# Attention and wave layer on one core: value matmuls one key tile at a time, overlapping PSUM bank ranges, and the layer norm's last step on VectorE

## What is computed

```python
def layernorm(x):                       # over the 256 columns, no gain or shift
    return (x - mean(x)) / sqrt(var(x) + 1e-5)

def attn(x):                            # 16 heads of 16, causal, rotary positions
    Q, K, V = split(x @ w_qkv); Q, K = rope(Q), rope(K)
    p = softmax(where(causal, Q @ K.T * 16 ** -0.5, -1e9))
    return (p @ V) @ w_proj + b_proj

def ffn(x):
    real = x @ cos(theta + theta_noise); imag = x @ sin(phi + phi_noise)
    return sqrt(real ** 2 + imag ** 2)

x = x + attn(layernorm(x))
x = x + ffn(layernorm(x))
```

## Time and profile before

| | |
|---|---|
| median of 3 runs | 2079.31 us (2078.74 to 2079.62) |
| the profiled execution | 2079.31 us, span from first to last instruction 2077.5 us |
| granted TensorE clock, mean | 0.992 |
| TensorE busy | 2033.7 us, 98% of the span |
| VectorE, ScalarE, GpSimd busy | 1486.1 us (72%), 1400.4 us (67%), 871.2 us (42%) |
| DMA | 159.91 MB, mean 77 GB/s |

### The profile page before, as it was taken

How to read it: one execution, slowest core, us unless ns; L and a number is a source line. 1 busy time by engine, 2 the same in 40 slices (tenths; PEclk the granted TensorE clock), 3 DMA queues, 4 the chain that set the end, 5 groups by cost and what they waited for, 6 DMA issues and landing times.

```text
span 2077.5 us, 39248 instructions
## 1 busy us (share of the span) xinstructions
PE 2033.7 (98%) x13184; PEld 883.4 (43%) x13184; DVE 1486.1 (72%) x2724; ACT 1400.4 (67%) x2705; POOL 871.2 (42%) x1336
## 2 busy tenths in 40 slices
PE   7999999999999999999999999999999999999998
PEld 5433344344443444444443444434444344434345
DVE  4766988877777777786777767787676877778322
ACT  2456667776667676776667676787666766676673
POOL 3335325453433535543363443447344343721242
PEclk9999999999999999999999999999999999999999
DMA  5314222222222322222232222333222222320221
GB/s 144 80 33 110 63 75 72 83 85 71 66 79 69 95 76 72 87 83 87 66 86 80 82 64 66 91 93 95 81 65 73 66 85 76 109 64 13 64 95 36
DMA packets 120553, 159.91 MB, mean 77 GB/s; under 512 B 30746, under 2 KB 82586, under 8 KB 120346
## 3 DMA queue, kind: packets, MB, share of 16 engines
q1 hardware_dynamic: 118480, 154.18, 25.6%
q10 hardware_dynamic: 1872, 3.21, 0.9%
HBM read 88.89 MB, written 50.85 MB: 67 GB/s over the span
## 4 chain that ended last, share of the span: by engine, by line
PE 85%; ACT 5%; issue 3%; POOL 2%; DMA 2%; DVE 2%; SPq 1%; ACTq 0%; POOLq 0%; DVEq 0%
PE banks L938 22%; PE banks L953 21%; PE banks L916 21%; PE banks L871 6%; PE banks L882 5%; PE banks L914 3%; PE banks L898 3%; PE banks L834 3%; ACT probs L1049 2%; DVE chunk_max L1195 2%; DMA stack_k<-split 1%; PE banks L961 1%; PE banks L823 1%; ACT inverse L1069 1%; POOL guess L1272 1%
## 5 line engine op out<-in xcount | busy, mean ns | idle before, releaser
L1195 DVE TENSOR_REDUCE chunk_max<-banks 128x1 f32<-128x512 f32 (+3 forms) x2240 | 1345.7, 667 | 416.2 <-PE banks L916 414.3
L1049 ACT ACTIVATE probs<-banks 128x512 f32<-128x512 f32 (+1 forms) x2240 | 1131.1, 600 | 394.5 <-PE banks L938 270.4
L916 PE MATMUL banks<-stack_k,stack_q 96*128 96x512 bf16 (+3 forms) x2560 | 749.7, 352 | 5.7 <-DVE chunk_max L1195 2.2
L938 PE MATMUL banks<-stack_q,stack_k 99*128 99x512 bf16 (+3 forms) x2560 | 730.5, 350 | 13.4 <-ACT probs L1049 9.2
L953 PE MATMUL banks<-probs,v_one 128*17 128x512 f32 (+3 forms) x5120 | 517.1, 531 | 0.4 <-POOL probs L1337 0.2
L938 PEld LDWEIGHTS banks<-stack_q,stack_k 99*128 99x128 bf16 x2560 | 232.0, 97 | 417.3 <-ACT probs L1049 263.1
L916 PEld LDWEIGHTS banks<-stack_k,stack_q 96*128 96x128 bf16 x2560 | 243.5, 98 | 242.3 <-DVE chunk_max L1195 89.7
L1337 POOL TENSOR_SCALAR_AFFINE_SELECT probs<-probs 128x512 f32<-128x512 f32 x256 | 161.0, 639 | 377.4 <-ACT probs L1049 376.0
L953 PEld LDWEIGHTS banks<-probs,v_one 128*17 128x17 f32 x5120 | 124.9, 97 | 289.9 <-issue 212.6
L914 PE MATMUL banks<-diag_mask,ident_bf 128*128 128x128 bf16 x1024 | 201.2, 223 | 5.4 <-DMA stack_k<-split 3.9
L1321 POOL TENSOR_SCALAR max_neg<-row_max 128x16 f32<-128x16 f32 x64 | 16.4, 257 | 360.6 <-DVE row_max L1204 356.6
(11 more groups left out here) (134 smaller groups left out, 1196.6 us busy)
## 6 DMA issues: line engine op xcount, KB each, us to landing
split<-parts SPq DMA_DIRECT2D x64, 384.0 KB, 2.7
stack_q<-split SPq DMA_DIRECT2D x384, 64.0 KB, 2.3
stack_k<-split SPq DMA_DIRECT2D x354, 64.0 KB, 2.2
sums<-o_raw SPq DMA_DIRECT2D x64, 256.0 KB, 2.1
rot<-raw SPq DMA_DIRECT2D x246, 64.0 KB, 2.0
xin<-x SPq DMA_DIRECT2D x16, 512.0 KB, 4.0
heads_t<-sums SPq DMA_DIRECT2D x26, 256.0 KB
mid<-x SPq DMA_DIRECT2D x13, 512.0 KB, 4.1
```

Source lines behind the costliest of these rows:

```text
L916: mm = nc.tensor.matmul(bank[:, n * wide:(n + 1) * wide], stack_q[u % 2][0:SPLIT_ROWS, t, h + n, j * P:(j + 1) * P], stack_k[u % 2][0:SPLI ...
L938: mm = nc.tensor.matmul(bank[:, a * wide:(a + 1) * wide], stack_k[u % 2][0:ROWS, j // SUB, first + a, (j % SUB) * P:(j % SUB + 1) * P], st ...
L1049: nc.scalar.activation(probs[:, g % PROBS, first:first + many, w0:SPAN], bank, ACT.Exp).then_inc(s_exp, 1)
L1195: nc.vector.tensor_reduce(to, bank[:, 0:count * wide].rearrange("p (h n) -> p h n", h=count), AX.X, ALU.max).then_inc(s_emptied["DVE"], 1)
```

## The change

Three things change together; the plan is then made anew from the same rules, so all queues come out in another order.

1. `VALUES` goes from 2 to 1: a `values` job covers one step, and the exponentials of step g are planned to wait for the values of step g-4 alone instead of the pair.
2. `SCORE_BANKS` goes from banks 0 to 2 to banks 0 to 3, `OTHER_BANKS` from 3 to 6 to 2 to 6. There are still seven banks in the ring; banks 2 and 3 may hold either kind.
3. The last step of both layer norms moves from ScalarE (scale and shift) to VectorE (subtract the mean, multiply by the inverse deviation). VectorE also adds the epsilon, so GpSimd has five operations a block instead of eight.

```diff
-VALUES = 2
+VALUES = 1
-STAT_OPS = 8
-ROOT_OPS = 8
+STAT_OPS = 9
+ROOT_OPS = 5
-SCORE_BANKS = range(0, 3)
-OTHER_BANKS = range(3, 7)
+SCORE_BANKS = range(0, 4)
+OTHER_BANKS = range(2, 7)
...
-            job(("stats", n), "DVE", 2.0, at, ...)
-            job(("dev", n), "POOL", 2.8, at, [("stats", n), ("apply", n - 1)])
-            job(("apply", n), "ACT", 1.35, at, [("dev", n)])
+            job(("stats", n), "DVE", 2.1, at, ...)
+            job(("dev", n), "POOL", 2.0, at, [("stats", n), ("apply", n - 1)])
+            job(("apply", n), "DVE", 1.4, at, [("dev", n)])
...
-                def normalise(n):
-                    half = n % 2
-                    act.wait_ge(s_root, ROOT_OPS * (n + 1))
-                    for j in range(SUB):
-                        ins = nc.scalar.activation(xin[:, half, j, :], xin[:, half, j, :], ACT.Identity, bias=shift[:, j:j + 1], scale=rstd[:, j:j + 1])
-                    ins.then_inc(s_xn, 1)
...
                 def block_stats(n):
                     half = n % 2
                     base = STAT_OPS * n
-                    if n:
-                        dve.wait_ge(s_stat, base)
...
+                    dve.wait_ge(s_stat, base + 8)
+                    nc.vector.tensor_scalar(variance[:, half, :], mv[:, half, :, 1], EPS, None, ALU.add).then_inc(s_stat, 1)
+
+                def normalise(n):
+                    half = n % 2
+                    dve.wait_ge(s_root, ROOT_OPS * (n + 1))
+                    for j in range(SUB):
+                        ins = nc.vector.tensor_scalar(xin[:, half, j, :], xin[:, half, j, :], mv[:, half, j, 0:1], rstd[:, j:j + 1],
+                                                      ALU.subtract, ALU.mult)
+                    ins.then_inc(s_xn, 1)
...
-                    nc.gpsimd.tensor_scalar(var, mean_var[:, :, 1], EPS, None, ALU.add).then_inc(chain, 1)
-                    nc.gpsimd.tensor_scalar(centre[:, :], mean_var[:, :, 0], -1.0, None, ALU.mult).then_inc(chain, 1)
...
-                    nc.gpsimd.tensor_tensor(shift[:, :], centre[:, :], result[:, :], ALU.mult).then_inc(chain, 1)
```

More of the change, by code:

```diff
@@ L224, in plan @@
             job(("xload", n), "SP", 0.45, at, [("xt", n - 2, 1), ("rot", 0, n - 2) if n < SPANS else begun(at - SLACK)], (4.8, 9.5)[n] if n < 2 else 4.2)
-            job(("stats", n), "DVE", 2.0, at, [("xload", n), ("apply", n - 2), *([("apply", 0)] if n == 1 else []), begun(at - SLACK)])
-            job(("dev", n), "POOL", 2.8, at, [("stats", n), ("apply", n - 1)])
-            job(("apply", n), "ACT", 1.35, at, [("dev", n)])
+            job(("stats", n), "DVE", 2.1, at, [("xload", n), ("apply", n - 2), *([("apply", 0)] if n == 1 else []), begun(at - SLACK)])
+            job(("dev", n), "POOL", 2.0, at, [("stats", n), ("apply", n - 1)])
+            job(("apply", n), "DVE", 1.4, at, [("dev", n)])
             for k in range(KT):
@@ L305, in plan @@
                     with_bank(("proj", n, a), ("proj", n, a), "DVE", 0.65, at + 0.1, [("out", ("lead", n, a))])
-            job(("stats3", n), "DVE", 2.0, at + 0.1, [("out", ("proj", n, 1)), ("apply3", n - 1)])
-            job(("dev3", n), "POOL", 2.8, at + 0.1, [("stats3", n), ("apply3", n - 1)])
-            job(("apply3", n), "ACT", 1.35, at + 0.1, [("dev3", n)])
+            job(("stats3", n), "DVE", 2.1, at + 0.1, [("out", ("proj", n, 1)), ("apply3", n - 1)])
+            job(("dev3", n), "POOL", 2.0, at + 0.1, [("stats3", n), ("apply3", n - 1)])
+            job(("apply3", n), "DVE", 1.4, at + 0.1, [("dev3", n)])
             for k in range(KT):
@@ L1096, in _ @@
                         lift(*name[1:])
[L1097 to L1100, removed]
                     elif name[0] == "sin":
@@ L1134, in block_stats3, with normalise3 @@
                         nc.vector.bn_aggr(mv3[:, j, :], stats3[:, j, :]).then_inc(s_stat3, 1)
+                    dve.wait_ge(s_stat3, base + 8)
+                    nc.vector.tensor_scalar(variance3[:, :], mv3[:, :, 1], EPS, None, ALU.add).then_inc(s_stat3, 1)
+                def normalise3(n):
+                    dve.wait_ge(s_root3, ROOT_OPS * (n + 1))
+                    for j in range(SUB):
+                        ins = nc.vector.tensor_scalar(normed3[finish_set(n)][:, j, :], mid[finish_set(n)][:, j, :], mv3[:, j, 0:1], rstd3[:, j:j + 1],
+                                                      ALU.subtract, ALU.mult)
+                    ins.then_inc(s_xn3, 1)
                 def invert(n):
@@ L1243, in _ @@
                         block_stats(name[1])
+                    elif kind == "apply":
+                        normalise(name[1])
                     elif kind == "rope":
@@ L1289, in deviation @@
                     pool.wait_ge(s_stat, STAT_OPS * (n + 1))
-                    inverse_deviation(ROOT_OPS * n, s_root, mv[:, n % 2, :, :], variance[:, n % 2, :], centre, guess, correction, rstd, shift)
+                    inverse_deviation(ROOT_OPS * n, s_root, variance[:, n % 2, :], guess, correction, rstd)
                 def deviation3(n):
```

23 lines of the change are left out of this document (9 added, 14 removed).

## The result

The changed kernel takes 2107.18 us (2105.7 to 2108.38, 4 runs) against 2079.47 us of the kernel before: ratio 1.0131, 95% interval 1.0113 to 1.0148. I had forecast 2051 us and a range of 2025 to 2100. The profiled execution took 2102.79 us with a span of 2101.0 us, 23.5 us over that of before.

A forecast was written before the change was run, and what follows sets the result against it. The prediction took TensorE's queue (columns, mode changes, short waits) to bound the kernel. From 2079.3 us, +36 mode changes, -57 waits, -7 apply off ScalarE, +3 apply on VectorE and -3 ends gave 2051 us, range 2025 to 2100.

The forecast's parts named there:

- What bounds the kernel: TensorE's queue sets the time: streamed columns, 50 us of four-column mode changes and 106 us of short waits.
- Mode changes, +36 us: TensorE: single-step values give 430 stretches instead of 249, 181 more at 0.20 us each.
- The drains win: Rival on TensorE: mode switches at nearly every step, 600 stretches, +70 us, sum +18, 2097 us; chance 0.20.
- Waits, -57 us: TensorE: shorter values stretches and flexible banks remove a little over half of 106 us of waits.
- The apply off ScalarE, -7 us: ScalarE: 28 apply bursts no longer block emptying score banks, saving 0.24 us each.
- The apply on VectorE, +3 us: VectorE: 0.33 us a piece, 48 us more load hidden by idle time; 0.1 us a block reaches TensorE.
- My cover: VectorE's 28% idle time and up to five banks before TensorE would hide the 48 us of added load.
- The ends, -3 us: Both ends: start -2 us by block 0's shorter chain, end -0.8 us by fewer fillers, which hold the path.
- VectorE becoming the bound: Rival on VectorE: in nine-tenths-busy slices 1.5 us more a block is uncovered, +10 us, 2089 us; chance 0.07.
- Three of the signs that I had named: Profile signs: tensor_scalar piece 0.33 us (0.6 means missized load), VectorE busy near 1534 us, waits near 100 us mean wrong.
- Two others: Profile signs: line 938's 714 waits for exponentials fall to about half; VectorE's wait for line 916 clearly under 414 us.

The follow-up runs named there:

- e4: Changed kernel with the apply put back on ScalarE, so VALUES = 1 and overlapping banks on the kernel before: 2074.9 us, 0.9970.
- e13: Kernel before with VALUES = 1 and TURN_COST = 0 in the plan, so mode changes count as free: 2119.6 us, 1.0180.
- e14: Kernel before, pairs of values kept, with TURN_COST = 0 in the plan: 2108.0 us, 1.0126.
- e3: Kernel before with only the last step of both layer norms moved to VectorE: 2117.6 us, 1.0182.
- e5: As e3, same queue order, but layer-norm tensor_scalar in accumulator form, leaving out the apply's multiplication: 2082.7 us, 1.0011 against the kernel before.
- e7: Whole change with the accumulator form of e5, same queue order, apply's multiplication left out: 2067.7 us, 0.9935 against the kernel before.
- e2: Kernel before with the overlapping bank ranges alone, two banks shared: 2095.7 us, 1.0073.
- e12: Kernel before with one bank shared, scores 0 to 3 and the rest 3 to 6: 2093.2 us, 1.0046.

## Why the prediction was wrong, point by point

**Where the 56 us lie.** The forecast was 28 us under the kernel before, the measurement is 28 us over it. Values and banks together were to give -21 us (+36 - 57) and gave -6 (e4). The apply with the ends was to give -7 (-7 + 3 - 3) and costs 32 to 37. So some 40 of the 56 us belong to the apply and some 15 to values and banks. Within those 15 us two larger errors partly cancel, which is luck: the waits fell by 3 us and not 57, and the mode changes cost some 6 us (31 stretches more in e4 at 0.20 us) and not 36.

**What bounds the kernel** was read rightly: TensorE's queue, with 50 us of mode changes and 100 us of waits beside its columns. e13 moved both of them, and its time followed.

**Mode changes, +36 us.** The price of 0.20 us is right (e13). The number was wrong: 285 stretches and not 430, 36 more instead of 181, some +7 us by that price. Steps merged at 2.2 to a stretch, not 1.5. The drains win, the rival with the greatest chance on the slow side, did not happen in the change, since the plan kept to long stretches; e13 shows that it would have.

**Waits, -57 us.** This term was wrong by the most, 54 us for values and banks alone (e4), and it was the only large one that pointed to a gain. Values alone took away 3 us of waits, values and banks together 3. I had put half of all waits down to stretches that last too long. e13 tests this: 338 more stretches save 31 us, 0.09 us a stretch, less than half of what each costs. At that rate the 36 stretches more of the change would save about 3 us; e14 shows that the waits can also rise with their number.

**The apply off ScalarE, -7 us.** Waits at the scores fell from 45 to 36 in e3 and to 40 in e5, so a gain of this size is plausible, and no run isolates it. With the apply on VectorE and not held, e7 is 7 us faster than e4, as much as the three terms for the apply give (-7 + 3 - 3), but e5 is 2 us slower than the kernel before: a close sum for one order of the queues and not for the other.

**The apply on VectorE, +3 us: the step that failed and turned the sign.** With everything that goes with it, it measured +37 us on the kernel before and +32 us on top of the rest. The 0.33 us itself was right for a piece that nothing holds (0.32 us from start to start), and so was the cover for plain load; what was missing is that GpSimd stops VectorE. The place to see it was "from the second 0.6 us; I take 0.33". I read 1189 ns for 512 elements as a length to average with, when the row itself asked a question: why should 512 elements take 1189 ns and 1024 take 683? The trace of before had the answer, and I did not look it up. Its timeline around that instruction, GpSimd and VectorE:

```profile
324.76 1.28 POOL L590 TENSOR_TENSOR crossed<-rot,sin_t 128x512 f32<-128x512 f32 x1
...
325.13 1.19 DVE L1232 TENSOR_SCALAR heads_t<-heads_t 128x512 f32<-128x512 f32 x1
...
326.12 1.33 POOL L592 TENSOR_TENSOR turned<-turned,crossed 128x512 f32<-128x512 f32 x1
...
326.85 1.16 DVE L1234 TENSOR_SCALAR heads_t<-heads_t 128x1024 f32<-128x1024 f32 x1
```

Both VectorE operations began while GpSimd was at a rotary product or sum, at 324.76 and 326.12, and ended 0.28 and 0.56 us after it. The one of 683 ns met no GpSimd operation. With this, I would have suspected that a piece's length depends on GpSimd, which is busy 42% of the time and has single operations of 2.4 us. My cover, "28% idle time" and "up to five banks between", was right for the load (e5: 63 us for 2 us) and wrong for the hold. At 868 us in the changed kernel TensorE filled its five banks in 1.44 us, and VectorE, held for 2.4 us in a burst that takes 1.4 us alone, had emptied the first of them only 2 us later.

**The ends, -3 us.** The opposite of what I said at the end: the apply came to the path by being held, with 0.84 us of idle time before the transpose. Without the hold its 1.4 us would have ended some 1.2 us before the fillers (an estimate from the lengths above).

**The rivals.** VectorE becoming the bound was my case for this engine, with a chance of 0.07 and 2089 us. Its place was right (the maxima behind the new work), its mechanism wrong, as I took it for a matter of total load. Three of the signs that I had named showed it: a piece near 0.6 us and more, VectorE far over 1534 us, the waits near or over 100 us. Two others pointed the other way and would have misled: the loads' waits for exponentials fell from 714 to 499, and VectorE's wait for line 916 fell from 414 to 344 us, as one would expect of an engine that counts as busy while it is held.

**What stays open.** Why overlapping banks lose 15 us with pairs of values and gain 4 us beside single steps, why the same longer duration makes one plan 10 us better and another 5 us worse, and why e14 costs 27 us. The waits rise with the losses (119, 122 and 118 us in e2, e12 and e14), but no run tells which placement causes them. Whether GpSimd is in turn held by VectorE was not tried by itself; its lengths show little of it (the rotary products of line 583 have a median of 1.27 us, as before, and one of the 62 sums of line 588 took 2.14 us). How much of the loss is the clock's is open, as said above. A whole apply on VectorE that is not held was not tried either, since the accumulator form leaves out the multiplication.

## What to carry to other kernels

Before moving work to VectorE, ask which of its instructions share a path with GpSimd, and look for rows of the same operation whose lengths do not fit their sizes; a mean hides it, and a short operation that is long is the sign. Idle time covers added load but not an interruption longer than the buffers last, so compare the longest hold with the banks in between and not with the idle share. A kernel whose order comes from a plan answers to small edits by several microseconds in either direction, 10 and 5 us here for one duration, which is luck and not insight: run each part alone, and in pairs, before giving it a cause.

## What the runs showed of the hardware that I had not expected

- A VectorE tensor_scalar on SBUF tensors waits for a running GpSimd operation: 399 to 422 ns for 256 float32 columns alone, up to 2443 ns beside it; 170 ns against up to 1236 ns for four elements. All 55 pieces of 256 columns that began during one ended after it, 54 of them by 0.14 to 0.15 us. scalar_tensor_tensor with two SBUF inputs does the same, 471 to 484 against up to 2572 ns.
- The accumulator form takes 522 to 540 ns for 256 columns (0.46 us from start to start) whatever GpSimd does, with another 0.08 us for reading the accumulator, overlapped. Its second operation is not applied to the output.
- One round trip into the four-column mode and back costs 0.20 us, by 338 of them in e13.
- TensorE's granted clock fell to half (1.2 GHz) for 3.4 or 6.8 us during or just after idle stretches of 1.0 to 2.8 us, four times between 200 and 1900 us in the changed kernel and five times in e3. Other idle stretches of the same length had no such fall.
